# Cross-attention and mixture-of-experts block on one core: key projection from the f16 high and low parts of context and weights, with the context loaded and split one step ahead

## The reference

```python
# x, ctx: (8, 512, 256) f32; 16 heads of width 16; softmax inside blocks of 64 positions
xn = layernorm(x)
q, k, v = xn @ Wq + bq, ctx @ Wk + bk, ctx @ Wv + bv      # 256 x 256 weights
attn = softmax(q k^T / sqrt(16), masked to blocks of 64)
x = x + (attn @ v) @ Wo + bo
z = layernorm(x)
gate = top 2 of softmax(z @ gate_w^T + bias) over 8 experts, normalized
ffn = sum over the two experts e of gate_e * (gelu(z @ up_e^T) @ down_e^T)   # width 1024
x = x + layernorm(ffn) + z
```

## Time and profile before

| | |
|---|---|
| median of 3 runs | 824.08 us (823.51 to 826.54) |
| the profiled execution | 823.3 us, its span 821.5 us |
| PE busy | 720.0 us (88%) |
| PEld, DVE, ACT, POOL busy | 79%, 65%, 44%, 54% |
| mean granted PE clock | 0.933 |

### The profile page before, as it was taken

How to read it: one execution, slowest core, us unless ns; L and a number is a source line. 1 busy time by engine, 2 the same in 40 slices (tenths; PEclk the granted TensorE clock), 3 DMA queues, 4 the chain that set the end, 5 groups by cost and what they waited for, 6 DMA issues and landing times.

```text
span 821.5 us, 20896 instructions
## 1 busy us (share of the span) xinstructions
PE 720.0 (88%) x6400; PEld 646.7 (79%) x6401; DVE 536.7 (65%) x1150; ACT 363.7 (44%) x657; POOL 442.4 (54%) x584
## 2 busy tenths in 40 slices
PE   4999999999999718699999999999999999999200
PEld 4899999999999514599899999988899999898200
DVE  4888888888888579455555555555555555555295
ACT  3877787777777403122222222222222222222284
POOL 3787887788787407524444344444443443432287
PEclk9999999999999955699999999999999999999755
DMA  4333333333332100111111111111111111110494
GB/s 157 111 110 117 109 116 107 117 104 119 103 121 85 41 7 0 52 40 53 53 51 45 45 51 45 45 51 51 51 46 47 48 45 45 51 38 27 160 319 161
DMA packets 39875, 64.54 MB, mean 79 GB/s; under 512 B 5408, under 2 KB 30240, under 8 KB 39840
## 3 DMA queue, kind: packets, MB, share of 16 engines
q1 hardware_dynamic: 31632, 42.37, 16.1%
q0 software_dynamic: 7488, 20.46, 7.8%
q10 hardware_dynamic: 720, 1.26, 0.5%
HBM read 45.46 MB, written 18.61 MB: 78 GB/s over the span
## 4 chain that ended last, share of the span: by engine, by line
PE 85%; DVE 5%; issue 3%; DMA 2%; POOL 2%; ACT 1%; SPq 1%; DVEq 0%; ACTq 0%; POOLq 0%
PE ps_a L531 25%; PE ps_b L545 25%; PE ps_b L434 6%; PE ps_a L391 4%; PE ps_b L401 4%; PE ps_c L413 3%; PE ps_c L418 3%; PE ps_a L469 3%; PE ps_a L456 2%; PE ps_c L499 2%; PE ps_c L515 2%; PE ps_a L480 1%; PE ps_c L379 1%; PE ps_a L444 1%; DMA resid<-x_in 1%
## 5 line engine op out<-in xcount | busy, mean ns | idle before, releaser
L531 PE MATMUL ps_a<-area,w_hi 128*128 128x256 f16 x1248 | 208.3, 274 | 1.7 <-DVE area L795 1.7
L545 PE MATMUL ps_b<-w_hi,area 128*128 x1248 | 206.4, 273 | 0.0
L1055 POOL DMA_INDIRECT y_rows<-area x78 | 78.1, 1001 | 209.2 <-ACT area L940 197.3
L531 PE MATMUL ps_a<-area,w_lo 128*128 128x256 f16 x624 | 171.0, 274 | 0.0
L545 PE MATMUL ps_b<-w_lo,area 128*128 x624 | 170.1, 273 | 0.0
L935 ACT ACTIVATE area<-ps_a 128x512 f32<-128x512 f32 x156 | 93.2, 597 | 142.6 <-PE ps_a L531 142.6
L531 PEld LDWEIGHTS ps_a<-area,w_hi 128*128 x1248 | 122.7, 98 | 16.3 <-issue 2.1
L545 PEld LDWEIGHTS ps_b<-w_hi,area 128*128 128x128 f16 x1248 | 122.1, 98 | 14.1
L793 DVE TENSOR_SCALAR area<-ps_c 128x512 f16<-128x512 f32 x39 | 27.0, 692 | 151.5 <-PE ps_c L515 151.5
L805 DVE SCALAR_TENSOR_TENSOR area<-area 128x512 f16<-128x512 f32 x156 | 108.4, 695 | 5.4
L940 ACT ACTIVATE area<-ps_b 128x512 f32<-128x512 f32 x39 | 23.3, 598 | 181.1 <-PE ps_b L545 181.1
(11 more groups left out here) (129 smaller groups left out, 1251.2 us busy)
## 6 DMA issues: line engine op xcount, KB each, us to landing
area<-weights SPq DMA_DIRECT2D x32, 512.0 KB, 3.3
w_hi<-y_rows SPq DMA_DIRECT2D x32, 256.0 KB, 4.6
resid<-x_in SPq DMA_DIRECT2D x32, 128.0 KB, 2.1
area<-ctx_t SPq DMA_DIRECT2D x32, 128.0 KB, 2.1
xn_rows<-area SPq DMA_DIRECT2D x32, 128.0 KB, 1.7
out<-w_lo SPq DMA_DIRECT2D x16, 256.0 KB, 2.8
area<-xn_rows,area POOLq DMA_INDIRECT x78, 2.8
y_rows<-area POOLq DMA_INDIRECT x78
```

The lines of the kernel that those rows point to most:

```text
L531: mm = pe.matmul(ps_h[:, q, (ic % 2) * SLOTS:(ic % 2 + 1) * SLOTS], w[:, bass.ds(first + (hc * I + ic * P), P)], r[b][:, hc, :], start=(n ...
L545: mm = pe.matmul(ps_y[:, b, v * D:(v + 1) * D], g[b][:, ic, v * P:(v + 1) * P], w[:, bass.ds(first + (EXPERT_COLS + ic * D), D)], start=(n ...
L1055: pool.indirect_dma_start(y_rows[:, :], bass.IndirectOffsetOnAxis(ap=didx[b][:, v:v + 1], axis=0), y_s[b][:, v * D:(v + 1) * D], None).the ...
```

## The change

The key projection becomes three f16 products, as the value projection is: `wk_hi` by `ctx_hi`, `wk_hi` by `ctx_lo`, `wk_lo` by `ctx_hi`. That takes 12 f16 matmuls of 128 columns for 4 f32 ones. The split of the context is therefore made one step earlier, tile i+2 in step i, and `ctx_hi` and `ctx_lo` have two buffers each; the load is of tile i+3. The key weights are loaded by a DMA of their own (into the buffer of the probabilities), scaled by 256 and split before step -2 of ACT. Keys come out too large by 64 x 256; their bias is multiplied by that factor once, and the scale of the exponential is divided by it. Some small tiles move into other tensors to make room; this changes no instruction's size.

```diff
-        wq_s, wk_s, wo_s = (... w_qk_s[:, 0:HC * D], w_qk_s[:, HC * D:2 * HC * D], wo_flat ...)
+        wq_s, wo_s = (... w_qk_s[:, 0:HC * D], wo_flat ...)
-        ctx_hi, ctx_lo = (carve(D, F16).rearrange("p (c n) -> p c n", c=HC) for _ in range(2))
+        wk_hi, wk_lo = (w_qk_s[:, HC * D + h * HC * D // 2:HC * D + (h + 1) * HC * D // 2].bitcast(F16).rearrange("p (c n) -> p c n", c=HC) for h in range(2))
+        ctx_hi, ctx_lo = ([carve(D, F16).rearrange("p (c n) -> p c n", c=HC) for _ in range(2)] for _ in range(2))
+        wk_flat = prob[:, 0:HC * D]
+        wk_s = wk_flat.rearrange("p (c n) -> p c n", c=HC)
...
# SP, step
-                t, half, b = here(j, u, 1)
+                t, half, b = here(j, u, 3)
                 if valid(t):
-                    since(sp, v_ps, t - 1)
+                    since(sp, ctx_lo_r, t - 1)
                     sp.dma_start(ctx[b], ctx_t[bass.ds(t, 1)].rearrange("a p c n -> p (a c) n")).then_inc(ctx_in[b], 16)
...
# PE, step, tile i+1
-                    pe.wait_ge(ctx_in[b], 16 * (half + 1))
+                    pe.wait_ge(ctx_lo_r, t + 1)
                     for c in range(HC):
+                        n = 0
                         for k in range(HC):
-                            mm = pe.matmul(ps_k[:, c, :], wk_s[:, k, c * P:(c + 1) * P], ctx[b][:, k, :],
-                                           start=(k == 0), stop=(k == HC - 1))
+                            for w, r in ((wk_hi, ctx_hi), (wk_hi, ctx_lo), (wk_lo, ctx_hi)):
+                                mm = pe.matmul(ps_k[:, c, :], w[:, k, c * P:(c + 1) * P], r[b][:, k, :],
+                                               start=(n == 0), stop=(n == 3 * HC - 1))
+                                n += 1
                     mm.then_inc(k_ps, 1)
...
# PE, before step -1
+            pe.wait_ge(wk_lo_r, 1)
             step(-1, 1)
...
# DVE, before step -1
+            dve.tensor_scalar(bk_s, bk_s, CTX_SCALE * W_SCALE, None, ALU.mult).then_inc(bk_scaled, 1)
+            dve.wait_ge(wk_hi_r, 1)
+            dve.tensor_tensor(wk_lo, wk_s, wk_hi, ALU.subtract).then_inc(wk_lo_r, 1)
+            dve.wait_ge(bk_scaled, 1)
             step(-1, 1)
...
# ACT, loads
-            act.dma_start(w_qk_s, w_qk).then_inc(qk_in, 16)
+            act.dma_start(w_qk_s[:, 0:HC * D], w_qk[:, 0:HC * D]).then_inc(qk_in, 16)
+            act.dma_start(wk_flat, w_qk[:, HC * D:2 * HC * D]).then_inc(wk_in, 16)
...
# ACT, step: the scaling of the context, now of tile i+2
-                t, half, b = here(j, u, 0)
+                t, half, b = here(j, u, 2)
                 if valid(t):
                     act.wait_ge(ctx_in[b], 16 * (half + 1))
-                    act.wait_ge(k_ps, t + 1)
                     act.activation(ctx[b], ctx[b], ACT.Copy, scale=CTX_SCALE).then_inc(ctx_scaled, 1)
...
-                t, half, b = here(j, u, 0)
-                if valid(t):
-                    act.wait_ge(ctx_scaled, t + 1)
-                    since(act, v_ps, t)
-                    since(act, ctx_lo_r, t)
-                    act.activation(ctx_hi, ctx[b], ACT.Copy).then_inc(ctx_hi_r, 1)
...
-                    act.activation(prob, prob, ACT.Exp, scale=DK ** -0.5).then_inc(p_r, 1)
+                    act.activation(prob, prob, ACT.Exp, scale=DK ** -0.5 / (CTX_SCALE * W_SCALE)).then_inc(p_r, 1)
...
# ACT, at the end of the step
+                t, half, b = here(j, u, 2)
+                if valid(t):
+                    act.wait_ge(ctx_scaled, t + 1)
+                    since(act, v_ps, t - 1)
+                    act.activation(ctx_hi[b], ctx[b], ACT.Copy).then_inc(ctx_hi_r, 1)
# ACT, before its first step
+            act.wait_ge(wk_in, 16)
+            act.activation(wk_s, wk_s, ACT.Copy, scale=W_SCALE).then_inc(wk_scaled, 1)
+            act.wait_ge(wk_scaled, 1)
+            act.activation(wk_hi, wk_s, ACT.Copy).then_inc(wk_hi_r, 1)
+            step(-1, 0)
             step(-1, 1)
...
# POOL, step: from before the query mask to behind w_lo
-                t, half, b = here(j, u, 0)
-                if valid(t):
-                    pool.wait_ge(ctx_hi_r, t + 1)
-                    since(pool, v_ps, t)
-                    pool.tensor_tensor(ctx_lo, ctx[b], ctx_hi, ALU.subtract).then_inc(ctx_lo_r, 1)
...
+                t, half, b = here(j, u, 2)
+                if valid(t):
+                    pool.wait_ge(ctx_hi_r, t + 1)
+                    since(pool, v_ps, t - 1)
+                    pool.tensor_tensor(ctx_lo[b], ctx[b], ctx_hi[b], ALU.subtract).then_inc(ctx_lo_r, 1)
```

More of the change, by code:

```diff
@@ L101, in program @@
         gate_bias = cst[:, C_GATE_B:C_END]
-        AREA = 11500
+        AREA = 11450
         area = sb("area", [P, AREA])
@@ L116, in program @@
         w_qk_s, wo_flat = carve(2 * HC * D), carve(HC * D)
-        wq_s, wk_s, wo_s = (w.rearrange("p (c n) -> p c n", c=HC) for w in (w_qk_s[:, 0:HC * D], w_qk_s[:, HC * D:2 * HC * D], wo_flat))
+        wq_s, wo_s = (w.rearrange("p (c n) -> p c n", c=HC) for w in (w_qk_s[:, 0:HC * D], wo_flat))
         bo_s = carve(D)
@@ L137, in program @@
         xn2 = carve(D)
[L138 to L141, removed]
+        row_max, o_sum = (slot_dest[:, h * PAIRS * NB:(h + 1) * PAIRS * NB].bitcast(F32) for h in range(2))
+        stats1, stats2 = (slot_token[:, h * 8:h * 8 + 6].bitcast(F32) for h in range(2))
+        mv1, mv2 = ([slot_token[:, 16 + 4 * h + 2 * i:18 + 4 * h + 2 * i].bitcast(F32) for i in range(2)] for h in range(2))
         ve1, ve2 = carve(1), carve(1)
@@ L187, in program @@
         c_ve, c_rs, c_nm = (carve(TILES) for _ in range(3))
-        neg_half, eps, warm = sb("neg_half", [P, CG]), sb("eps", [P, CG]), sb("warm", [P, 1])
+        few = sb("few", [P, 2 * CG + 1])
+        neg_half, eps, warm = few[:, 0:CG], few[:, CG:2 * CG], few[:, 2 * CG:2 * CG + 1]
         ps_a = es.enter_context(nc.psum_tensor("ps_a", [P, 4, 512], F32))
@@ L221, in program @@
             sem(n) for n in ("wv_scaled", "wv_hi_r", "wv_lo_r", "ctx_scaled", "ctx_hi_r", "ctx_lo_r"))
+        wk_in, bk_scaled = sem("wk_in"), sem("bk_scaled")
+        wk_scaled, wk_hi_r, wk_lo_r = sem("wk_scaled"), sem("wk_hi_r"), sem("wk_lo_r")
         q_r, qb_r, k_ps, k_r, v_ps, v_r = (sem(n) for n in ("q_r", "qb_r", "k_ps", "k_r", "v_ps", "v_r"))
@@ L450, in step @@
                 if valid(t):
-                    pe.wait_ge(ctx_lo_r, t + 1)
                     since(pe, v_r, 2 * t)
@@ L454, in step @@
                     for k in range(HC):
-                        for c, w in ((ctx_hi, wv_hi), (ctx_hi, wv_lo), (ctx_lo, wv_hi)):
+                        for c, w in ((ctx_hi[b], wv_hi), (ctx_hi[b], wv_lo), (ctx_lo[b], wv_hi)):
                             mm = pe.matmul(ps_v, c[:, k, :], w[:, k, :], start=(n == 0), stop=(n == 3 * HC - 1))
```

## The result

The changed kernel takes 819.25 us in the median of 5 runs (818.69 to 819.41), the kernel before 824.08 (823.51 to 826.54). Here both medians are of 5 runs; the table of the kernel before gives the median of its first 3, which is the same. The ratio is 0.9932, with a 95% interval of 0.9916 to 0.9948: 0.7% faster. The profiled execution took 818.69 us (span 816.9), that of before 823.3.

The account below looks back on a forecast made before the run. PE was taken to bound the kernel, its step setting the time. 823.3 - 6.6 (key projection) + 1.1 (start) = 817.8 us for the profiled execution, 818.6 for the median; range 816.2 to 825.5.

Parts of the forecast that it names:

- Part 1: Key projection on PE: 12 f16 matmuls at 56 ns, 0.67 for 0.89 us, -0.22 us a step.
- Part 2: How often the key projection's saving counts: 30 of 32 times on PE's path, 30 x -0.22 = -6.6 us.
- Part 3: Work moved on ACT, POOL and SP in the loop: costs nothing, bounds 0 and +0.1 us a step.
- The two covers: Slack hiding moved work: ACT's high part 0.2 us before its copy; POOL's low part 1.8 us before PE wants it.
- Part 4: The start, first transpose waiting for the key weights' split: +1.1 us, bounds +0.3 and +2.2.
- rival C: At the start ACT and DVE prepare weights in series while first tiles wait: costs 3.5 us, time 821.0; chance 0.10.
- Rival A: Ring of SP's store, load of x and DVE holds steps at mean 8.16 us: time 823.4, no change; chance 0.20.
- Rival B: In the key projection f16 weight loads can't overlap, 98 ns a matmul: +0.29 us a step, 833.9 us; chance 0.08.
- its mild form: Key projection's weight loads overlap each other but not the columns, 73 ns a matmul: 825.0 us, no change; chance 0.06.

Follow-up runs that it names:

- e2: Changed kernel without the third product of the key projection (low weights by high context), 8 f16 matmuls for 12: 812.06 us, ratio 0.9854.
- e1: Changed kernel with the key projection in f32 again (8 records, on the query's operands), order and splits kept: 825.36 us, ratio 1.002.
- e6: Kernel before with a small copy on ACT ahead of its first wait, so its table loads early: 822.41 us, ratio 0.9981.
- e11: The changed kernel as it is, timed again in a later job: 820.21 us, ratio 0.9947.
- e7: Changed kernel with POOL's low part of the context back at its old place, ahead of the query mask in the same step: 870.95 us.
- e9: Changed kernel with PE's wait for the key weights' low part moved from its first transpose to the first key projection: 817.94 us.
- e4: Changed kernel with the load of the key weights issued first on ACT's queue: 816.45 us, interval 0.9880 to 0.9919.
- e8: Changed kernel with early ACT table load, key weights issued first, and x of tiles 0 and 1 issued ahead of any context: 816.15 us.
- e3: Changed kernel with a small copy on ACT that loads its table before the key weights are there: 817.91 us.
- e10: Changed kernel with early table load, key weights first, x of two tiles first, and PE's low-part wait at the key projection: 815.17 us.

## Why the prediction was right, and where not

The forecast was 818.6 us, in a range of 816.2 to 825.5, with faster at 0.56. Measured were 819.25 and 820.21, both inside the range; by the prediction's own bound for faster, 820.0, the first is faster and the second just isn't.

- **Part 1, the key projection:** right. 56 ns and 0.67 us were forecast and measured, in the change and in e2. The trace differs from the Trainium skill (TensorE: Matmul & The Clock Gate, section "Back-to-back issue gap") here: 12 pairs of load and matmul at 128 columns, one behind the other, ran at 56 ns each, the value that the page gives for a matmul by itself, and not at 81.
- **Part 2, 30 times -0.22:** right for the regular step, 8.00 for 8.22, and shown from both sides, by e1 (back to 8.21) and e2 (on to 7.78). The sum over the steps, -7.97, is larger than the -6.6 forecast. 28 steps at 0.22 give 6.2; some 1.0 more are irregular steps of the one profiled execution of before, which e6, in the old order too, didn't have; and the first three steps, of which the forecast counted two, gave 0.87. In e11's profile the sum was -6.35.
- **Part 3, the other engines at nothing:** right. The two covers were as thin as said: ACT's copy now waits 0.6 us in all over 200 us of trace, POOL's inverse square root 1.5 us. In the timeline of the change the low part ends at 151.56 (150.88 + 0.68), and the key projection that needs it begins at 153.71: 2.1 us to spare for the 1.8 forecast. e7 shows what stands behind this cover: 9.75 us a step.
- **Part 4, the start, +1.1 us:** this term was wrong. It was +3.45 at the first scores. The step that failed is "as two halves it lands at about 5.1". The key weights released ACT at 8.01, 2.9 later, and at 7.10 to 8.36 in the six other profiles with the same issue order. The rest of that sum held: from there to the query projection 4.79 us (12.80 - 8.01), for 5.1, and the cold key projection took 1.49 us for 1.91, the 0.4 given back. The cost was that of rival C (3.5), by another cause: not the work in series on ACT and DVE, but the landing. The range of the term, up to +2.2, did not hold it. Its upper end named a cause of this kind, two more context tiles in flight, but at 1.1 us more for a delay of 2.9.
- **The sum:** 817.8 was forecast for the profiled execution, 818.69 came. Two errors stand against each other, +2.35 in the start and about -1.4 in the steps. That they nearly cancel is luck: 1.0 of the second hangs on one execution of the kernel before, and 0.54 on the first step, whose scores ran at full pace. With the steps as forecast and the start as measured, the sum is 823.3 - 6.6 + 3.45 = 820.2 for the profiled execution and 821.0 for the median. The direction was thus less safe than the first result makes it look.
- **Rival A (x too late):** fell for the changed kernel. DVE waits for PE, and so even with steps of 7.78 (e2). **Rival B (the weight load sets the pace)** and its mild form: fell by the 56 ns.

## What to carry to other kernels

Where one engine is busy without a gap, count its records by their measured pace, and the saving per step is safe as long as no other engine's round is as long; what moves beside it costs nothing only while its cover lasts, so ask for each moved operation what it would cost without the cover (here 0.22 us gained a step, 1.5 lost). Work that is added to the start is paid once in full, and its size hangs on which of the first transfers lands when: take landing times for each transfer by its place in the issue order, with a margin (one order gave 7.10 to 8.36 us here), not from another order. One profiled execution holds steps that another doesn't, so regular steps should be compared apart from irregular ones, and a sum of terms from one profile is no surer than its least sure stretch.

## What the runs showed of the hardware

- Splitting a transfer in two on one queue did not keep its time. The 512 KB were down 3.8 us after their issue; of the two 256 KB halves, issued at 1.18 and 1.67, the second released ACT only at 8.01. In seven profiles with this order it did so between 7.10 (e1) and 8.36 us (e9). Over both the profile gives a median of 5.0 us from issue to landing:

```profile
area<-w_qk ACTq DMA_DIRECT2D x2, 256.0 KB, 5.0
```

  Issued first on its queue, that half was there at 4.07 (e4). From 2 to 8 us the DMA engines' busy share was 0.89 in the change and 0.95 in the kernel before, so they were nearly full in both and whatever came earlier pushed something later. Which of the others delayed it (x of tile 1 landed late as well, DVE was released by it at 7.02) was not separated.
- DVE's normalization of 128x256 f32 elements took 0.83 us where POOL's split began in the same moment (e7) and 0.41 where it didn't, after the change. A rule of the Trainium skill (SBUF — State Buffer, section "Who interferes with whom") says that such a DVE operation and a POOL operation can shut each other out for an instruction's length. The trace agrees in kind, not in length: POOL's operation took 0.67 us, and DVE's grew by 0.42. It lay off the path and gave no time in the regular steps (e1).
- The 16 records of the first scores took 1.16 us in the change, but 2.08 in the kernel before, e4, e8 and e11, about twice the 1.09 of later steps, and 1.55, 1.47 and 1.87 in e3, e9 and e10. The granted clock accounts for it, but the column of the stretches misleads: it says 1.00 from 16 to 18 us in the change and in e4 alike. The trace's own clock records begin at the upper level (1.00, 2.4 GHz) at 16.7 us in the change, behind PE's work from 12.8 to 16.1 and ahead of the first scores. In the kernel before they begin at 18.3, in e4 at 21.8, in e8 at 18.1 and in e11 at 23.6, all later than the first scores' start, with PE at work. Ahead of the first record the column says 1.00 too, yet the matmuls run at half pace: there it is no reading. In the change the clock fell to the lower level at 20.1, PE having stood idle from 16.1 to 18.4, and rose again at 23.5, as its stretches show (the columns are those of the earlier trace rows):

```profile
18.00:20.00 2.00, 1.58 (x19) 1.32 (x20) 0.87 (x4) 1.08 (x3) 1.60 (x4) 1.00 0.06 8
20.00:24.00 4.00, 4.00 (x28) 3.68 (x28) 3.68 (x6) 2.67 (x3) 1.13 (x2) 0.57 0.59 193
```

  In e3, e9 and e10 the same fall, at 17.7, 18.8 and 14.2, lies inside the first scores (from 17.03, 18.07 and 13.88). Its place isn't set by how early the start is, so an earlier start can be partly paid back in slower first scores, as in e4, or not.
